# A cross-attention kernel: each score matmul of four heads becomes two of two heads, on separate rows of the TensorE array

## The reference

```python
q = heads(hidden_states @ W_q)
scores_t = jnp.einsum('bhsd,bhtd->bhst', q, k_t) * attn_scale      # 73 text tokens
probs_t = softmax(scores_t);  text_out = probs_t @ v_t
attn_scores = jnp.einsum('bhsd,bhnd->bhsn', q, k_ip) * attn_scale  # 4 image tokens
qsem = l2norm(einsum('bhst,bte->bhse', probs_t, text_ehs))
sem = einsum('bhse,bne->bhsn', qsem, l2norm(ip_ehs))
probs_ip = softmax(attn_scores + 0.5 * sem) * spatial_mask
out = (text_out + probs_ip @ v_ip) @ W_out + b_out + residual
```

## Time and profile before

| | |
|---|---|
| median of 3 runs | 1110.35 us (1110.32 to 1112.25) |
| the profiled execution | 1114.77 us, span 1112.9 us |
| mean granted clock of TensorE | 0.974 |
| busy share of the span | PE 92%, PEld 75%, DVE 76%, ACT 61%, POOL 52% |
| matmuls | 7829, of which 960 are score products (L979) |

### The profile page before, as it was taken

The page is one execution under the profiler, slowest core; times in us unless marked ns, Lnnn a source line. Parts: engine busy times, 40 slices in busy tenths (PEclk is TensorE's granted clock), DMA queues, the critical chain, the costliest instruction groups (busy, mean ns, idle before and its releaser), DMA issues.

```text
span 1112.9 us, 23936 instructions
## 1 busy us (share of the span) xinstructions
PE 1026.0 (92%) x7829; PEld 839.5 (75%) x7829; DVE 840.6 (76%) x2400; ACT 676.1 (61%) x1979; POOL 575.0 (52%) x1535
## 2 busy tenths in 40 slices
PE   6994587899999999999999999999999999999978
PEld 5872466778787878787887878787878787877856
DVE  3145277888888888888888888788878888887862
ACT  1134376766676666766766766676776676676630
POOL 0000255655565665656555656565656656655650
PEclk9798798999999999999999999999999999999989
DMA  9498556877869887968879778878698778877662
GB/s 292 137 210 184 133 112 143 150 161 148 184 130 194 177 166 137 195 136 155 164 159 194 150 161 163 179 138 185 128 199 164 174 146 177 144 143 139 136 115 81
DMA packets 465941, 177.63 MB, mean 160 GB/s; under 512 B 433417, under 2 KB 442917, under 8 KB 465817
## 3 DMA queue, kind: packets, MB, share of 16 engines
q1 hardware_dynamic: 465817, 176.10, 76.6%
HBM read 43.15 MB, written 28.05 MB: 64 GB/s over the span
## 4 chain that ended last, share of the span: by engine, by line
PE 72%; DVE 9%; DMA 4%; issue 2%; POOL 2%; ACT 1%; SPq 1%; DVEq 0%; POOLq 0%
PE ps_O L1003 27%; PE ps_Q L1037 21%; PE ps_U L1023 11%; PE ps_S L979 10%; DMA pts<-ph 3%; PE ps_M L1051 2%; DVE pr L917 1%; DVE n L929 1%; DVE f L933 1%; DVE x_in L866 1%; DVE attn L942 1%; PE ps_M L1065 1%; DVE f L949 1%; DMA x_in<-in_x_dram 1%; ACT pr L770 1%
## 5 line engine op out<-in xcount | busy, mean ns | idle before, releaser
L770 ACT ACTIVATE pr<-ps_S,bias 128x73 f32<-128x73 f32 x1280 | 288.7, 338 | 171.9 <-DVE bias L881 171.9
L847 POOL TENSOR_TENSOR ph<-pr,ph 128x440 f16<-128x440 f32 x320 | 228.2, 734 | 241.2 <-ACT ph L782 241.0
L1003 PE MATMUL ps_O<-wo_hi,aT 128*128 128x320 f16 x1280 | 295.5, 302 | 25.2 <-DVE x_in L866 25.2
L1037 PE MATMUL ps_Q<-xT,wq_hi 128*128 128x512 f32 x800 | 279.7, 415 | 6.2 <-DVE qT L854 6.1
L782 ACT ACTIVATE ph<-pr 128x584 f16<-128x584 f32 x320 | 204.2, 688 | 7.6 <-DMA pts<-ph 2.6
L1003 PE MATMUL ps_O<-wo_lo,aT 128*128 128x320 f16 x640 | 192.2, 300 | 0.0
L1003 PEld LDWEIGHTS ps_O<-wo_hi,aT 128*128 128x128 f16 x1280 | 125.4, 98 | 86.8 <-DVE x_in L866 29.5
L1023 PE MATMUL ps_U<-xm,pts 128*128 128x110 f16 (+1 forms) x2560 | 158.7, 214 | 17.3 <-DMA pts<-ph 16.9
L979 PE MATMUL ps_S<-kbd,qT 128*128 128x308 f32 x960 | 171.0, 314 | 1.1 <-ACT pr L770 1.0
L1037 PEld LDWEIGHTS ps_Q<-xT,wq_hi 128*128 128x128 f32 x800 | 145.9, 190 | 33.5 <-DVE qT L854 8.0
L874 DVE TENSOR_REDUCE smax<-ps_S 128x8 f32<-128x584 f32 x160 | 121.9, 762 | 62.0 <-PE ps_S L979 61.6
(11 more groups left out here) (163 smaller groups left out, 1380.1 us busy)
## 6 DMA issues: line engine op xcount, KB each, us to landing
x_in<-in_x_dram SPq DMA_DIRECT2D x16, 1280.0 KB, 6.7
out_dram<-x_in SPq DMA_DIRECT2D x64, 320.0 KB, 3.1
w_k<-in_L_xattn_W_k_dram SPq DMA_DIRECT2D x5, 512.0 KB, 9.1
w_ip<-in_L_xattn_W_k_ip_dram SPq DMA_DIRECT2D x1, 2560.0 KB, 11.9
w_v<-in_L_xattn_W_v_dram SPq DMA_DIRECT2D x1, 2560.0 KB, 19.8
w_ip<-in_L_xattn_W_v_ip_dram SPq DMA_DIRECT2D x1, 2560.0 KB, 10.3
pts<-ph SPq DMA_TRANSPOSE x160, 4.4
xm<-x_d SPq DMA_DIRECT2D x20, 110.0 KB
```

The costliest lines, as they stand in the source:

```text
L770: last = nc.scalar.activation(pr[p % P_RING][:, j, h, :], sc[:, j, h, 0:T], ACT.Exp, bias=bias[p % 2][:, j, h:h + 1], scale=SCALE)
L847: nc.gpsimd.tensor_tensor(lo, full[:, :, t0:t1], one[:, :, 0, t0:t1], ALU.subtract).then_inc(pl_ready, 1)
L1003: last = nc.tensor.matmul(o_bank[half % 2][:, 0:HALF], stationary, moving, start=(k, a, b_) == O_MMS[0], stop=(k, a, b_) == O_MMS[-1])
L1037: last = nc.tensor.matmul(ps_Q[:], wq[a][:, c, k * P:(k + 1) * P], xT[(CC * i + c) % XT_RING][b_][:], start=(c, a, b_) == Q_MMS[0], stop=( ...
```

## The change

Each score matmul of four heads over 128 partitions becomes two, of two heads each: the first with partitions 0 to 63 of the weights and of `kbd`, and columns 0 to 153, the second with partitions 64 to 127 and columns 154 to 307. The blocks that are left out of the sum are zeros in `kbd`. The two write to different PSUM banks: bank `gh` now holds heads 2 `gh` and 2 `gh` + 1 of both subtiles, where bank `j` held all four heads of subtile `j`. The readers of the scores, and the layouts of `smax` and `bias`, follow: (half of the heads, subtile, head) in place of (subtile, head). Counts and sizes of their instructions are unchanged. Waits and signals are unchanged.

```diff
+    HB = HG // 2
...
-    smax = [sb(f"smax{i}", [P, 2, HG], F32) for i in range(2)]
-    bias = [sb(f"bias{i}", [P, 2, HG], F32) for i in range(2)]
+    smax = [sb(f"smax{i}", [P, 2, 2, HB], F32) for i in range(2)]
+    bias = [sb(f"bias{i}", [P, 2, 2, HB], F32) for i in range(2)]
...
-    sc = ps_S2[:].rearrange("p (j w) -> p j w", j=2)[:, :, 0:GK].rearrange("p j (h t) -> p j h t", h=HG)
+    sc = ps_S2[:].rearrange("p (g w) -> p g w", g=2)[:, :, 0:GK].rearrange("p g (j h t) -> p g j h t", j=2, h=HB)
...
                     for j in range(2):
                         for h in range(HG):
-                            last = nc.scalar.activation(pr[p % P_RING][:, j, h, :], sc[:, j, h, 0:T], ACT.Exp,
-                                                        bias=bias[p % 2][:, j, h:h + 1], scale=SCALE)
+                            gh, hh = divmod(h, HB)
+                            last = nc.scalar.activation(pr[p % P_RING][:, j, h, :], sc[:, gh, j, hh, 0:T], ACT.Exp,
+                                                        bias=bias[p % 2][:, gh, j, hh:hh + 1], scale=SCALE)
...
-                    nc.vector.tensor_reduce(smax[p % 2][:], sc[:, :, :, 0:T], AX.X, ALU.max).then_inc(max_done, 1)
+                    nc.vector.tensor_reduce(smax[p % 2][:], sc[:, :, :, :, 0:T], AX.X, ALU.max).then_inc(max_done, 1)
...
-                    nc.vector.tensor_copy(s_ip[slot % SIP_RING][:, subs], sc[:, :, :, T:T_ALL]).then_inc(s_read, 1)
+                    nc.vector.tensor_copy(s_ip[slot % SIP_RING][:, subs].rearrange("p j (g h) n -> p g j h n", g=2),
+                                          sc[:, :, :, :, T:T_ALL]).then_inc(s_read, 1)
...
                         for a, m in PASSES:
-                            last = nc.tensor.matmul(g["ps_S"][j][:, 0:GK], qT[slot % 2][a][:, q * P:(q + 1) * P],
-                                                    kbd[:, m, slot % CC, :], start=(a, m) == PASSES[0],
-                                                    stop=(a, m) == PASSES[-1])
+                            for gh in range(2):
+                                r, w = slice(gh * HB * DH, (gh + 1) * HB * DH), HB * T_ALL
+                                last = nc.tensor.matmul(g["ps_S"][gh][:, j * w:(j + 1) * w],
+                                                        qT[slot % 2][a][r, q * P:(q + 1) * P],
+                                                        kbd[r, m, slot % CC, gh * w:(gh + 1) * w],
+                                                        start=(a, m) == PASSES[0], stop=(a, m) == PASSES[-1])
                     last.then_inc(s_ready, 1)
```

## The result

The changed kernel takes 1130.55 us (median of 4 runs, 1122.15 to 1135.39) against 1111.07 us before (4 runs, 1110.32 to 1112.25): 1.0166 times as long, 95% interval 1.0104 to 1.0228. It is slower, by 19.5 us where 10.5 were forecast.

The account below looks back on a forecast made before the run. TensorE (PE) was taken to bound the kernel, 92% busy, the score stage 0.84 us a pair. Profiled 1114.8 us plus 10.5 for the longer stage, less 4.4 to the median, gave 1121 us; whole range 1083 to 1195.

Parts of the forecast that it names:

- the forecast's own range: Range of the main case, exposed loads at the score stage's edges with overlapping loads inside: 1102 to 1144 us, chance 0.29.
- the sum: Score stage 0.188 + 5 x 0.112 + 0.070 + 0.098 = 0.916 us against 0.84, +10.5 us in all.
- The interior: Inside the score stage: six rounds 0.112 us apart, the loads of both halves overlapping.
- The price of serial loads: Rival for the score stage: loads one after the other, 12 x 0.112 = 1.34 us; 1179 to 1230 us, chance 0.20.
- The edges: Switches between 128-row and 64-row products around the score stage: one exposed load each at full duration, no tail.
- the front edge: From last query product to scores: first score load exposed, 0.112 to 0.188 us, 0.188 in the sum.
- the back edge: From scores to output products: first f16 output load exposed, 0.049 to 0.098 us, 0.098 in the sum.
- a whole tail of 0.163: Rival: array runs empty at both score-stage edges, 0.163 us each; stage 1.24 us, 1165 to 1174 us, chance 0.14.
- The share: Part of a score-stage change that shows in the time: 0.86 to 1 of its size over 160 pairs.
- The readers: Maximum reduction, image score copy and exponentials: priced at nothing, at most 15 ns a pair, 2.4 us on VectorE.
- The clock: Rival: granted clock falls where loads fill PE; eight pairs at half clock cost 45 us, chance 0.03.

Follow-up runs that it names:

- the score loads in turn: Changed kernel with all six score products of rows 0 to 63 first, then all six of rows 64 to 127: 1155.36 us, ratio 1.0399.
- the narrow tall products: Changed kernel with its 12 score products of 154 columns using all 128 rows each: 1174.67 us, ratio 1.057.
- the repeat: The changed kernel measured once more, no edit: 1130.32 us (6 runs), ratio 1.0181.
- before with the additional product: Kernel before plus an unread product of 128 rows and 16 columns between the two subtiles of a pair: 1134.51 us, ratio 1.0205.
- the tall float16 kernel: Kernel before with score queries and keys as float16 high and low parts, products of 128 rows and 308 columns: 1112.14 us, ratio 0.9994.
- the float16 kernel with the tall pair: Changed kernel with float16 score parts, but 128-row products in the one pair per tile before the wait for x_in: 1093.2 us, ratio 0.9825.
- the float16 split: Changed kernel with score queries and keys as float16 high and low parts instead of float32r: 1099.34 us, ratio 0.9869.
- the changed kernel with the additional product: Changed kernel plus an unread product of 128 rows and 16 columns between the two subtiles of a pair: 1172.16 us, ratio 1.0538.

## Why the prediction was right, and where it was small

The kernel became slower by its edges, as forecast, and the time lies within the forecast's own range. Of the 19.5 us the longer stages make 10.35 in the 130 pairs of the loop that can be compared; 4 to 5 are falls of the clock, which the sum did not have; about 4 are not located.

**The interior.** Right. Six rounds, 0.11 us apart, the loads of both halves in flight together; the score loads in turn and the narrow tall products show what it costs when they are not (0.112 us for each load). The price of serial loads, 12 x 0.112, was borne out by the tall products; it was not the case at hand. The Trainium skill, TensorEngine Tiling (Array Packing), section Key Properties, has different tiles loading and multiplying in parallel. These traces agree: two loads end within 0.19 us.

**The edges.** The sum was right, 0.92 us of stage in the text and 0.92 in the trace (from 500.94 + 0.24 us, where the last query product has streamed, to 502.10), but its parts were put wrongly. I took the exposed loads at full duration and no emptying of the array. At the front the trace has the score load starting 0.32 us after the last query product, some 0.08 us after that has streamed its 0.24 us and 0.08 us before its recorded end. At the back it has the last two score products at

```profile
501.89 0.28 PE L984 MATMUL ps_S<-kbd,qT 64*128 64x154 f32 x2
```

At the rate of before, 0.070 us for 154 columns, they have streamed at 501.96, and the first output load starts at 502.09, 0.13 us later and 0.08 before their recorded end, 502.17. From the first round at 501.27 to the last it is 0.62 us, 0.06 more than five rounds of 0.112. So the front edge costs 0.08 + 0.06 us, where I had 0.188, and the back edge 0.13, where I had 0.098: both wait for a good part of the tail, but not for all of it, and of the load at the front only 0.06 us shows. That the two errors cancel and the sum comes out at 0.92 is luck.

The Trainium skill, TensorEngine Tiling (Array Packing), section Key Properties, has a change of the tiling mode drain TensorE. The late loads agree with it; they come 0.08 and 0.13 us late, where the rival had a whole tail of 0.163.

**The share.** I let 0.86 of the stage arrive. In the loop 0.08 x 130 = 10.4 us of stage stand against 10.35 us of time, 2.0 of them waits for `pts`: nearly all of it arrived. At that rate 160 pairs would cost 12.7 us.

**The readers.** Right: L876, L879 and L772 kept their times.

**The clock.** This is the term that was too small. I gave it 0.03 as a rival and nothing in the sum. It did not come as the rival had it, in a stretch filled with loads, but behind a wait. In the repeat three falls came on top: from the first to the last of these waits 15.2 us more than before, of which 10.35 are there without falls and 4.4 are the falls.

What brings the falls can be read by setting all the profiles beside each other. Where the score stage ahead of the wait has 128 rows, none of 56 waits of 1.11 to 1.66 us is followed by one: 14 each in before, in before with the additional product, in the tall float16 kernel and in the float16 kernel with the tall pair (the other kernels with a tall stage there wait 1.12 us or less, and have none either). Where it has half-height products, 9 of 55 are: none in the profiled after, three in the repeat, three in the float16 split and three of 13 with the additional product, where the waits are as short as 0.76 to 1.23 us. The first line is a wait of the tall float16 kernel, without a fall; the other two are one of the changed kernel with the additional product, and the stretch behind it:

```profile
403.31 0.31 PE L1003 MATMUL ps_O<-wo_hi,aT 128*128 128x320 f16 x1 [1.62 <-DVE x_in L866]
...
481.60 0.32 PE L1012 MATMUL ps_O<-wo_hi,aT 128*128 128x320 f16 x1 [1.14 <-DVE x_in L868]
...
481.80:485.10 3.30, 3.30 (x14) 0.50 1.12 336
```

So the length of the wait alone does not explain the falls, and the stage ahead of it matters. With the halves in turn (waits of 0.93 to 1.26 us) and with the products issued twice (0.77 to 0.79) there was none. Behind longer waits there are falls with tall stages too, as behind 2.35 us at 1059.73 us in before. What it is in the half-height stage that does it, no run tells apart.

**Unsettled.** About 4 of the 19.5 us. The profiled executions of before and of the repeat differ by 16.0 us of span; the rest is that the profiled before, 1114.77 us, lies over its median, and no profile of a faster execution of before was taken. The first of the waits comes at 230.01 us there and at 229.92 in the repeat, but at 226.35 in the profiled after, which had a granted clock of 0.89 from 0 to 210 us where the other two had 0.88: these 3.6 us are why the profiled after is only 7.4 us over the profiled before. How far the medians of before (1107 to 1117 us in single runs, with clocks from 0.980 to 0.969) are set by the clock in the prologue is open. So is the rest of the 21.9 us for 160 additional products in the kernel before: at 0.12 us a pair they make 19.

## What to carry to other kernels

Products on separate rows of the array do run side by side, loads included, but each switch between half-height and full-height products costs 0.13 to 0.15 us here in float32r and about 0.09 in float16 (0.60 us of stage less six rounds of 0.07, for two); count the rounds between two switches before splitting, and see whether the loads or the streaming set a round. Weights of float32r need 0.11 us a load and left 0.17 us of gain for 0.25 to 0.3 us of edges; in float16 the same split won. Look also at what stands right ahead of the engine's one long wait: here half-height products there cost the clock in some tiles, and a longer stage of 128 rows cost the loop nothing.

## What the runs showed that I had not expected

A float32r load of 64 rows is no shorter than one of 128 (188 ns both), but two on different rows start within the same 0.01 us. Loads of the second half began while products of the first were still queued (12 loads in 1.03 us when issued six and six). And a kernel's clock can fall after a wait that it had before without falling, once the stage ahead of the wait has half-height products: 3 falls in the profiled repeat, none in the profiled execution of the same kernel at 1122 us.
